# Scratch region, weight slabs, split y and weighted h placed on multiples of 128 bytes

## Chip, core and metric

The kernel runs on one core of one Trainium2 chip. The metric is the device time of one execution in microseconds, the median over runs.

## What is computed

A convolution of width 3 over two sequences of 2048 tokens and 1024 features gives 768 features; blockwise causal attention (blocks of 128 tokens, 16 heads of 64) works on them; a projection brings the result back to 1024 features, which is added to the input and normed. Then comes a dense layer of 1024x1024 with eight gated low-rank experts, again added and normed. All of it is in fp32. Cut to what matters:

```python
x = conv_general_dilated(inputs, conv_w, padding='SAME') + conv_b      # 1024 -> 768
q, k, v = split(x, 3)                    # 256 each, in blocks of 128 tokens
p = softmax(where(causal, (q@wq+bq)/8 @ (k@wk+bk).T, -1e9))
o = (p @ (v@wv+bv)) @ wo + bo
x = layernorm(inputs + o @ proj_w + proj_b)

base = x @ W_base.T + b_base
gate = softmax(x @ W_gate.T) - sigmoid(x @ W_thr.T + b_thr) / 8
weights = gate * (gate >= 0);  weights /= sum(weights)
h = einsum('nd,erd->ner', x, A)
out = layernorm(x + base + 2 * einsum('ner,ne,eor->no', h, weights, B))
```

## The kernel before

Every product is made of three fp32r matmuls (`PASSES`, line 64): each operand is split into a high part (HI, a copy in fp32r) and a low part (LO, the difference), and HI x HI, HI x LO and LO x HI are summed in one PSUM bank. The first operand of a matmul call is the one that the array holds (an LDWEIGHTS of its own), the second is the moving one, which is streamed through. TensorE runs one long stream in three stages:

1. **Convolution** (line 657). 12 sweeps of a minimal-filtering scheme over 1024-token tiles; 3456 matmuls of 256 columns. Held: the weights `w` in the arena `weights`. Moving: `x_split`, 1 KB a row, in the scratch region.
2. **Attention** (lines 1168, 1187, 1201, 1226, 1213, 1236), eight tiles of 512 tokens by eight head pairs, software-pipelined. Line 1187 makes K (bank h) and Q (bank a) with both operands in the arena; line 1236 (`add_out`) streams `heads_out`, which lies in scratch; line 1201 reads `q_and_k` and line 1226 `probs_T` and `v_heads`, all in scratch.
3. **Feed-forward** (`ffn_phase`, windows over 32 blocks of 128 tokens). A block takes 24 matmuls of each of the column groups 896 to 1161 (266 columns, banks e and h), 0 to 511 (banks c and f) and 512 to 895 (384 columns, banks d and g), all on line 1592: three passes over eight slabs `wf[kc]`. Held is `x1T` (arena), moving is the slab. Line 776 projects y: held `y_split`, moving `wp` (arena). Line 1609 applies the experts: held `h_weighted_T`, moving `wb` (arena). Lines 1582 and 1601 are transposes.

The order is written out by hand in each engine's program. SBUF is laid out by hand too. The arena `weights` starts at byte 16,512 of each partition, a multiple of 128, and `x1T`, `wp`, `wb` and the attention weights lie in it on multiples of 512 bytes from its start. `conv_tile`, `features_out`, `causal_mask` and `identity` start 96 bytes past a multiple of 128, `v_bias_rows` 32 past.

The scratch region starts at the next multiple of 32 after those (`self.base` in `AttentionStart`), which is byte 145,728: 64 bytes past a multiple of 128. `at(name, ...)` puts a tile at a byte offset in it. Nearly all offsets are multiples of 128, so most scratch tiles start 64 bytes past such a multiple; `y_split` and `proj_b_rows` start 32 past one, `weight_stage2` 96 past one.

A slab `wf[kc]` holds HI and then LO, each of `WCOLS` = 1162 columns or 4648 bytes, which is 40 bytes more than a multiple of 128. Six slabs follow each other in the arena, two (`late_weights`) in scratch. So the start of a moving read runs through many residues modulo 128: HI parts are on multiples of 16 bytes, LO parts 8 bytes past one. In slab 0 HI is on a multiple of 128 and LO 40 bytes past one. The offsets of the column groups (0, 512, 896 columns) are multiples of 128 bytes.

The LO parts of the slabs are made by GpSimd (line 956) and VectorE, the HI parts by ScalarE, once each.

Of the kernel before, what the change touches and what calls it, by code (L numbers as in the profile page):

```python
# [8 lines left out]
F32 = mybir.dt.float32  # L9
F32R = mybir.dt.float32r  # L10
# [4 lines left out]
P = 128  # L15
BATCH, SEQ, DM = 2, 2048, 1024
# [15 lines left out]
KC = WB // P  # L32
HP = HEADS // 2
XS = 3
WCOLS = DM + ER + EXPERTS + 2
GATE0 = DM + ER

BANKS = ((0, 512), (512, 896), (896, WCOLS))
QUAD = 4
# [7 lines left out]
ARENA = CC * CHUNK  # L47
MASK_ROWS = P // QUAD
MASK_STORES = QUAD
SCRATCH = 20880  # L50
SMALL = 80992
SCORE_SMALL = 81152
Phase = namedtuple("Phase", "sync gpsimd scalar vector tensor")
# [13 lines left out]
class AttentionStart:  # L67
# [9 lines left out]
    def __init__(self, ctx, nc):  # L77
        def sb(name, shape, dt):
            return ctx.enter_context(nc.sbuf_tensor(name, shape, dt))

        def sem(name):
            return ctx.enter_context(nc.semaphore(name))

        NW, TILE = self.NW, CF * ST
        self.banks = [ctx.enter_context(nc.psum_tensor(f"bank{chr(97 + i)}", [P, ST], F32)) for i in range(8)]
        self.arena = sb("weights", [P, ARENA], F32R)
        self.stages = sb("weight_stage", [P, 2 * WCOLS], F32)
        self.stage = self.stages[:, 0:NW]
        self.craw = sb("conv_tile", [P, CF, ST], F32)
        self.out = sb("features_out", [P, KC, ST], F32)  # L90
        self.mask = sb("causal_mask", [P, P], F32)
        self.ident = sb("identity", [P, P], F32)
        self.bq, self.bk = sb("q_bias", [P, HP], F32), sb("k_bias", [P, HP], F32)
        self.bv, self.bo = sb("v_bias_rows", [P, HE], F32), sb("o_bias", [P, KC], F32)

        self.start = [2 * NW * n for n in range(3)] + [6 * NW + 2 * TILE]
        self.w = [self.arena[:, a:a + 2 * NW].rearrange("p (i n) -> p i n", i=2) for a in self.start]
        self.cs = self.arena[:, 6 * NW:6 * NW + 2 * TILE].rearrange("p (i f n) -> p i f n", i=2, f=CF)

        self.bias_loaded = sem("attn_bias_loaded")  # L100
        self.wv_loaded, self.stage_loaded = sem("wv_loaded"), sem("weight_stage_loaded")
        self.w_hi, self.w_lo = sem("attn_w_hi"), sem("attn_w_lo")
        self.zeroed, self.masks = sem("attn_zeroed"), sem("attn_masks")
        self.c_loaded = sem("conv_tile_loaded")
        self.c_hi, self.c_lo = sem("conv_tile_hi"), sem("conv_tile_lo")
        self.stored = sem("stored")
        self.y_stored = [sem(f"conv_y_stored{i}") for i in range(2)]
        self.evac, self.fin_done = sem("conv_evacuated"), sem("conv_finished")

        self.base = (nc.sbuf_base + 31) // 32 * 32  # L110
        sb("scratch", [P, SCRATCH], F32)
        self.nc = nc

    def at(self, name, shape, dt, offset):

        assert 0 <= offset and offset + 4 * math.prod(shape[1:]) <= 4 * SCRATCH, name
        return self.nc.alloc_sbuf_tensor_at(name, shape, dt, offset=self.base + offset)
# [582 lines left out]
class FfnStart:  # L700
# [8 lines left out]
    def __init__(self, ctx, nc, attn, proj_w, ffn_w, lora_b):  # L709
        def sem(name):  # L710
            return ctx.enter_context(nc.semaphore(name))

        def parts(a, n):
            return attn.arena[:, a:a + 2 * n].rearrange("p (i n) -> p i n", i=2)


        qk = attn.at("q_and_k", [P, 2, 2, ST], F32, 0)
        self.k, self.q = qk[:, 0, :, :], qk[:, 1, :, :]
        late = attn.at("late_weights", [P, self.LATE * 2 * WCOLS], F32R, 45056)
        second, kept = attn.start[1], CC - self.LATE  # L720
        self.wp = [parts(attn.start[attn.WV] + 2 * DM * k, DM) for k in range(KC)]
        self.wf = [parts(second + 2 * WCOLS * k, WCOLS) for k in range(kept)]
        self.wf += [late[:, 2 * WCOLS * k:2 * WCOLS * (k + 1)].rearrange("p (i n) -> p i n", i=2) for k in range(self.LATE)]
        self.wb = parts(attn.start[attn.WO] + 2 * attn.NW, DM)

        wo = attn.start[attn.WO]
        self.x1T = attn.arena[:, wo:wo + 4 * DM].rearrange("p (i h k n) -> p i h k n", i=2, h=2, k=CC)
        self.stage = [attn.stages[:, i * WCOLS:(i + 1) * WCOLS] for i in range(2)]
        self.stage.append(attn.at("weight_stage2", [P, WCOLS], F32, 63648)[:])

        f = [(ffn_w[k], self.wf[k], WCOLS) for k in range(CC)]
        p = [(proj_w[k], self.wp[k], DM) for k in range(KC)]
        self.weights = [(lora_b, self.wb, DM)] + p + f
        self.AFTER_V, self.AFTER_QK = 1, 1 + KC
        self.KEPT = len(self.weights) - self.LATE

        raw = attn.craw[:].rearrange("p f n -> p (f n)")
        self.xt = raw[:, 0:2 * DM].rearrange("p (i n) -> p i n", i=2)
        self.yr = raw[:, 2 * DM:2 * DM + 2 * KC * P].rearrange("p (i k n) -> p i k n", i=2, k=KC)
        self.ys = attn.at("y_split", [P, 2, 2, KC, P], F32R, 68320)  # L740
        self.pb = attn.at("proj_b_rows", [P, DM], F32, 72416)

        self.w_loaded = [sem(f"ffn_w_loaded{i}") for i in range(STAGES)]
        self.w_hi = sem("ffn_w_hi")
        self.w_lo = [sem(f"ffn_w_lo{n}") for n in range(len(self.weights))]
        self.pb_loaded = sem("proj_b_loaded")
        self.x_loaded = [sem(f"x_tile_loaded{i}") for i in range(2)]
        self.y_loaded = [sem(f"y_loaded{i}") for i in range(2)]
        self.xb_ready = sem("x_plus_bias_ready")
        self.y_hi, self.y_lo = sem("y_hi"), sem("y_lo")  # L750
        self.attn_stored = attn.stored
        self.proj_done = sem("proj_done")
        self.res1_ready = sem("res1_ready")


        small = attn.at("ln_small", [P, 34], F32, SMALL)
        self.stats = small[:, 0:24].rearrange("p (k h n) -> p k h n", k=2, h=2)
        self.mv = small[:, 24:28].rearrange("p (k n) -> p k n", k=2)
        self.var_eps, self.rstd = small[:, 28:30], small[:, 30:32]
        self.minus_half, self.eps = small[:, 32:33], small[:, 33:34]  # L760
        self.consts = sem("ln_consts_ready")
        self.ln_step = [sem(f"ln{k + 1}_step") for k in range(2)]
        self.var_ready = [sem(f"ln{k + 1}_var_ready") for k in range(2)]
        self.rstd_ready = [sem(f"ln{k + 1}_rstd_ready") for k in range(2)]
        self.stats_seen = sem("ln_stats_seen")
        self.x1_ready = sem("x1_ready")
        self.first_x1 = attn.bv
# [529 lines left out]
def ffn_phase(nc, x, yT, attn, ffn, b_base, b_thr, out):  # L1297

    with ExitStack() as ctx:
# [20 lines left out]
        wts = attn.at("gate_weights", [P, EXPERTS], F32, 33536)  # L1320
        wsum = attn.at("gate_sum", [P, 3], F32, 33568)
        hw = attn.at("h_weighted", [P, ER], F32, 33600)
        hT = attn.at("h_weighted_T", [P, 2, P], F32R, 34112)
        ps_a = attn.banks[0:2]
        ps_f = [attn.banks[2:5], attn.banks[5:8]]
        HT0 = LAST
# [309 lines left out]
def build(nc, ins, out):  # L1636
    convT = nc.dram_tensor("convT_scratch", [NST, P, CF, ST], F32).ap()
    yT = nc.dram_tensor("yT_scratch", [P, KC, TOK], F32).ap()
    with ExitStack() as ctx:
        attn = AttentionStart(ctx, nc)  # L1640
        ffn = FfnStart(ctx, nc, attn, ins["proj_w"], ins["ffn_w"], ins["lora_b"])
        with ExitStack() as both:
# [27 lines left out]
            def _(pe):  # L1670
                conv.tensor(pe)
                attention.tensor(pe)

        ffn_phase(nc, ins["x"], TileColumns(yT, P), attn, ffn, ins["b_base"], ins["b_thr"], out)


# [59 lines left out]
```

## Time and profile before

| | |
|---|---|
| median of 3 runs | 1572.31 us (1571.24 to 1580.3) |
| span of the profiled execution | 1572.8 us |
| PE busy | 1541.9 us, 98% |
| PEld (weight loads) busy | 1375.7 us, 87% |
| DVE / ACT / POOL busy | 1181.8 / 610.3 / 256.3 us |
| matmuls | 10816 |
| DMA engines' time, queue q1 | 31.5% of 16 engines' span |

PE is TensorE's matmul stream and PEld its weight loads. Matmul durations overlap each other; the distance from one start to the next is what the stream takes. The chain of waits is the sequence of work that ended last, followed back from the end.

### The profile page before, as it was taken

The numbers are of one execution on the slowest core, as the hardware profiler recorded it, in microseconds if no ns is written. First come the engines' busy times: TensorE is split into PE (matmuls) and PEld (weight loads), VectorE is DVE, ScalarE is ACT, GpSimd is POOL, SyncE is SP. The second block draws the span as 40 slices with busy tenths as digits, with TensorE's granted clock in tenths as the row PEclk, the third lists the DMA queues.
The fourth block names the chain that finished last, engine by engine and source line by source line (L and its number), as shares of the span: only waits on it lengthen the run. The fifth ranks groups of instructions, "written<-read, shape, count | busy, mean of one in ns | idle before, by whom it ended". The sixth has DMA issues, their size and how long they took to land. (4 is left out here: it accounts for less than half of the span.)

```text
span 1572.8 us, 29280 instructions
## 1 busy us (share of the span) xinstructions
PE 1541.9 (98%) x10816; PEld 1375.7 (87%) x10816; DVE 1181.8 (75%) x2792; ACT 610.3 (39%) x1732; POOL 256.3 (16%) x227
## 2 busy tenths in 40 slices
PE   7999999999999999999999999999999999999997
PEld 7999999999878888888888887898988999989987
DVE  8859967887876666666666677787788888788875
ACT  4224223322466767676676677211111111111110
POOL 0000000000000101010000113433333333333331
PEclk9999999999999999999999999999999999999999
DMA  8987774678810100101010222312211112211111
GB/s 323 370 308 272 257 256 166 240 279 282 280 68 1 55 20 34 53 0 53 0 53 0 76 93 77 108 61 74 76 61 60 60 60 75 75 60 60 60 55 44
DMA packets 55301, 181.05 MB, mean 115 GB/s; under 512 B 5568, under 2 KB 13888, under 8 KB 48704
## 3 DMA queue, kind: packets, MB, share of 16 engines
q1 hardware_dynamic: 53504, 173.81, 31.5%
q10 hardware_dynamic: 1728, 6.29, 1.0%
q8 instruction: 47, 0.77, 0.2%
q14 instruction: 22, 0.18, 0.0%
HBM read 125.49 MB, written 54.53 MB: 114 GB/s over the span
## 5 line engine op out<-in xcount | busy, mean ns | idle before, releaser
L976 ACT ACTIVATE scores_and_probs<-scores_and_probs,score_neg_max 128x128 f32<-128x128 f32 x512 | 198.0, 391 | 2.1 <-DVE score_neg_max L1077 2.1
L943 POOL TENSOR_TENSOR weights<-conv_tile,weights 128x1024 fp32r<-128x1024 f32 x14 | 35.7, 2552 | 860.7 <-ACT weights L962 775.7
L1072 DVE CUSTOM_DVE_ANT_0 scores_and_probs<-bankb,causal_mask 128x128 f32<-128x128 f32 x256 | 59.2, 288 | 114.6 <-PE bankc L1201 114.2
L1428 ACT ACTIVATE gate_exp<-h_and_gate,gate_neg_max 128x8 f32<-128x8 f32 x32 | 9.7, 302 | 347.9 <-DVE gate_neg_max L1503 347.9
L380 ACT ACTIVATE x_split<-x_planes 128x1024 fp32r<-128x1024 f32 x47 | 49.9, 1061 | 169.6 <-PE bankf L657 126.7
L1168 PE MATMUL bankg<-weights 128*128 128x512 f32 x378 | 103.2, 408 | 0.6 <-DVE v_heads L1062 0.5
L1187 PE MATMUL bankh<-weights 128*128 128x512 f32 x384 | 99.0, 393 | 1.7 <-DVE probs_T L1090 1.7
L1187 PE MATMUL banka<-weights 128*128 128x512 f32 x384 | 98.3, 391 | 0.8
L976 ACT ACTIVATION_READ_ACCUMULATOR scores_and_probs<-scores_and_probs,score_neg_max 128x1 f32 x512 | 97.5, 190 | 0.0
L511 DVE TENSOR_TENSOR x_split<-x_planes,x_split 128x1024 fp32r<-128x1024 f32 x47 | 57.4, 1222 | 49.8 <-ACT x_split L380 49.8
L657 PE MATMUL banka<-x_split,weights 128*128 128x256 f32 x576 | 77.8, 283 | 13.2 <-DVE weights L615 8.7
L1187 PEld LDWEIGHTS bankh<-weights 128*128 128x128 f32 x384 | 71.6, 188 | 19.6 <-DVE probs_T L1090 2.9
L1187 PEld LDWEIGHTS banka<-weights 128*128 128x128 f32 x384 | 71.5, 188 | 18.6 <-POOL weights L943 3.4
L793 DVE BATCH_NORM_STATS2 ln_small<-residual_sum 128x6 f32<-128x512 f32 x126 | 81.1, 686 | 5.9 <-DVE residual_sum L787 4.6
L657 PEld LDWEIGHTS banka<-x_split,weights 128*128 128x128 f32 x576 | 72.1, 192 | 14.0 <-issue 12.0
L1084 DVE TENSOR_TENSOR scores_and_probs<-scores_and_probs,prob_inv_sum 128x1024 f32<-128x1024 f32 x64 | 80.4, 1256 | 2.2
L1201 PEld LDWEIGHTS bankb<-q_and_k 64*128 64x128 f32 x512 | 61.7, 187 | 22.6 <-issue 22.6
L1168 PEld LDWEIGHTS bankg<-weights 128*128 128x128 f32 x378 | 66.3, 189 | 12.3 <-DVE v_heads L1062 1.2
L802 DVE TENSOR_SCALAR out_tile<-residual_sum,ln_small 128x1024 f32<-128x1024 f32 x32 | 76.0, 2376 | 1.0 <-POOL ln_small L809 1.0
L657 PE MATMUL bankb<-x_split,weights 128*128 128x256 f32 x576 | 76.7, 281 | 0.0
L657 PE MATMUL bankc<-x_split,weights 128*128 128x256 f32 x576 | 75.7, 278 | 0.0
L657 PE MATMUL banke<-x_split,weights 128*128 128x256 f32 x576 | 75.5, 278 | 0.0
(244 smaller groups left out, 3885.0 us busy)
## 6 DMA issues: line engine op xcount, KB each, us to landing
x_raw<-in_xT SPq DMA_DIRECT2D x31, 1028.0 KB, 7.1
conv_tile<-in_x SPq DMA_DIRECT2D x32, 512.0 KB, 3.6
out<-out_tile SPq DMA_DIRECT2D x32, 512.0 KB, 2.7
conv_tile<-convT_scratch SPq DMA_DIRECT2D x16, 768.0 KB, 6.5
ce_scratch<-conv_l SPq DMA_DIRECT2D x16, 512.0 KB, 7.5
x_planes<-ce_scratch SPq DMA_DIRECT2D x16, 512.0 KB, 4.9
conv_y<-in_conv_w SPq DMA_DIRECT2D x6, 1152.0 KB, 6.5
convT_scratch<-conv_y SPq DMA_DIRECT2D x12, 512.0 KB, 6.1
```

Of the source, the lines that this page charges most:

```text
L380: nc.scalar.activation(xs[:, j % XS, HI], T[:, j % 2, 0:2], ACT.Copy).then_inc(x_hi, 1)
L511: nc.vector.tensor_tensor(xs[:, j % XS, LO], T[:, j % 2, 0:2], xs[:, j % XS, HI].bitcast(F32), ALU.subtract).then_inc(x_lo, 1)
L657: last = nc.tensor.matmul(acc[f][:, k, :], w[:, c, a, k, f * P:(f + 1) * P], xs[:, j % XS, b, k, c % CPG, :], start=(c == 0 and k == 0 and ...
L793: nc.vector.bn_stats(self.stats[:, k, h, :], src[:, h * ST:(h + 1) * ST]).then_inc(step, 1)
L802: nc.vector.tensor_scalar(dst, src, self.mv[:, k, 0:1], self.rstd[:, k:k + 1], ALU.subtract, ALU.mult).then_inc(ready, 1)
L943: nc.gpsimd.tensor_tensor(cs[:, LO, a:b, :], craw[:, a:b, :], cs[:, HI, a:b, :].bitcast(F32), ALU.subtract).then_inc(c_lo, 1)
L976: last = nc.scalar.activation(probs[:, s % 2, i, :], probs[:, s % 2, i, :], ACT.Exp, bias=ntop[:, s % 2, i:i + 1], scale=SCORE_SCALE, accu ...
L1072: last = nc.vector.tensor_tensor_reduce(out=probs[:, s % 2, i, :], in0=ps_s[h][:, n * P:(n + 1) * P], in1=mask[:], scale=1.0, scalar=LOWES ...
L1084: nc.vector.tensor_tensor(probs[:, s % 2, :, :], probs[:, s % 2, :, :], inv[:, s % 2, :].unsqueeze(2).broadcast_to([P, 2 * BLK, P]), ALU.m ...
L1168: last = nc.tensor.matmul(bank[:], cs[:, a, V[0] + kc, b * P:(b + 1) * P], wqkv(attn.WV, c, kc, cols), start=(i == 0), stop=(i == 5))
L1187: last = nc.tensor.matmul(out[:], wqkv(weight, a, kc, slice(s * P, (s + 1) * P)), cs[:, c, part[0] + kc, :], start=(i == 0), stop=(i == 5))
L1201: last = nc.tensor.matmul(ps_s[j][:, cols], q[rows(j), s % 2, cols], k[rows(j), s % 2, cols], start=True, stop=True)
```

## The change

`self.base` is rounded up to a multiple of 128: it becomes byte 145,792, and every scratch tile moves up by 64 bytes. The slabs' parts get a pitch `WPITCH` of 1184 columns (4736 bytes, 37 times 128), of which the first 1162 are used, so that HI and LO of all eight slabs start on multiples of 128. `weight_stage2`, `y_split` and `proj_b_rows` move up because the late slabs are longer, to multiples of 128. `h_weighted_T` moves by 64 bytes relative to the region, and so stays on a multiple of 128. `v_heads`, `q_and_k`, `probs_T`, `heads_out`, `x_split` and the other tiles that were 64 bytes past a multiple of 128 are on one now; a few small ones (`score_neg_max`, `h_weighted`, `gate_inverses`) were on one and are 64 past it now. `conv_tile`, `identity` and `v_bias_rows` stay. No engine's list of instructions differs: same operations, shapes, order and waits.

```diff
@@ -34,6 +34,8 @@
+LINE = 128
+WPITCH = (4 * WCOLS + LINE - 1) // LINE * LINE // 4
@@ -47,7 +49,7 @@
-SCRATCH = 20880
+SCRATCH = 20864
@@ -107,8 +109,8 @@
-        self.base = (nc.sbuf_base + 31) // 32 * 32
-        sb("scratch", [P, SCRATCH], F32)
+        self.base = (nc.sbuf_base + LINE - 1) // LINE * LINE
+        sb("scratch", [P, SCRATCH + LINE // 4], F32)
@@ -716,17 +718,20 @@
-        late = attn.at("late_weights", [P, self.LATE * 2 * WCOLS], F32R, 45056)
+        def slab(region, k):
+            return region[:, 2 * WPITCH * k:2 * WPITCH * (k + 1)].rearrange("p (i n) -> p i n", i=2)[:, :, 0:WCOLS]
+
+        late = attn.at("late_weights", [P, self.LATE * 2 * WPITCH], F32R, 45056)
         second, kept = attn.start[1], CC - self.LATE
-        self.wf = [parts(second + 2 * WCOLS * k, WCOLS) for k in range(kept)]
-        self.wf += [late[:, 2 * WCOLS * k:2 * WCOLS * (k + 1)].rearrange("p (i n) -> p i n", i=2) for k in range(self.LATE)]
+        assert second + 2 * WPITCH * kept <= attn.start[attn.WO]
+        self.wf = [slab(attn.arena[:, second:], k) for k in range(kept)] + [slab(late, k) for k in range(self.LATE)]
-        self.stage.append(attn.at("weight_stage2", [P, WCOLS], F32, 63648)[:])
+        self.stage.append(attn.at("weight_stage2", [P, WCOLS], F32, 64000)[:])
@@ -737,8 +742,8 @@
-        self.ys = attn.at("y_split", [P, 2, 2, KC, P], F32R, 68320)
-        self.pb = attn.at("proj_b_rows", [P, DM], F32, 72416)
+        self.ys = attn.at("y_split", [P, 2, 2, KC, P], F32R, 68736)
+        self.pb = attn.at("proj_b_rows", [P, DM], F32, 72832)
@@ -1320,7 +1325,7 @@
-        hT = attn.at("h_weighted_T", [P, 2, P], F32R, 34112)
+        hT = attn.at("h_weighted_T", [P, 2, P], F32R, 34176)
```

## Rows read from the trace of the kernel before

**Rows 1.** The page: busy time and share of the span, then TensorE's granted clock.

```profile
PE 1541.9 (98%) x10816; PEld 1375.7 (87%) x10816; DVE 1181.8 (75%) x2792; ACT 610.3 (39%) x1732; POOL 256.3 (16%) x227
...
PEclk9999999999999999999999999999999999999999
```

**Rows 2.** Waits of PE: who was waited for, total us, times, longest us.

```profile
PE banka L657 <- DVE weights L615: 8.7, 1, 8.7
PE banka L1582 <- PEq L1642: 3.3, 1, 3.3
PE banka L657 <- ACT conv_m L414: 3.2, 1, 3.2
PE bankd L1226 <- DVE heads_out L1094: 2.3, 1, 2.3
```

**Rows 3.** The chain of waits inside one feed-forward block: start us, us, what.

```profile
1173.72 3.04 PE banke L1592 x24
1176.75 5.55 PE bankc L1592 x24
...
1185.39 2.09 PE bankd L1592 x12
1187.48 1.40 PE banka L776 x6
1188.88 1.39 PE bankb L776 x6
1190.28 0.70 PE bankc L1609 x3
1190.97 0.53 PE bankd L1609 x3
```

**Rows 4.** Timeline of PE in attention: start us, us (overlapping), line, operation.

```profile
599.92 0.86 PE L1236 MATMUL banke<-heads_out,weights 128*128 128x512 f32 x3
600.62 0.86 PE L1236 MATMUL bankf<-heads_out,weights 128*128 128x512 f32 x3
601.32 1.54 PE L1187 MATMUL bankh<-weights 128*128 128x512 f32 x6
602.70 1.52 PE L1187 MATMUL banka<-weights 128*128 128x512 f32 x6
```

**Rows 5.** Instructions of lines 1592 and 1609: duration ns min/median/max.

```profile
L1592 PE MATMUL bankc<-weights x288: 389/394/400, 996.0 to 1541.7; 128*128 128x512 f32 x144
L1592 PE MATMUL bankd<-weights x288: 332/337/423, 1002.3 to 1547.3; 128*128 128x384 f32 x144
L1592 PE MATMUL bankd<-late_weights,weights x96: 331/334/338, 1005.7 to 1548.3; 128*128 128x384 f32 x96
L1609 PE MATMUL bankc<-weights,h_weighted_T x48: 389/395/398, 1009.5 to 1549.0; 128*128 128x512 f32 x48
```

**Rows 6.** Windows over two stretches of the convolution, line 657: PE busy (matmuls), clock, DMA.

```profile
45.00:145.00 100.00, 100.00 (x851) 1.00 0.83 311
175.00:275.00 100.00, 100.00 (x885) 1.00 0.67 240
```

**Rows 7.** Timeline of PE around an early wait of the convolution.

```profile
17.02 0.84 PE L657 MATMUL banke<-x_split,weights 128*128 128x256 f32 x6
17.70 0.84 PE L657 MATMUL bankf<-x_split,weights 128*128 128x256 f32 x6
19.12 0.97 PE L657 MATMUL banka<-x_split,weights 128*128 128x256 f32 x6 [0.58 <-DVE x_split L511]
19.93 0.87 PE L657 MATMUL bankb<-x_split,weights 128*128 128x256 f32 x6
20.64 0.87 PE L657 MATMUL bankc<-x_split,weights 128*128 128x256 f32 x6
```

**Rows 8.** Groups by line and shape on the other engines: busy us, mean ns | idle before.

```profile
L983 ACT ACTIVATE probs_T<-banka 128x512 f32<-128x512 f32 x64 | 38.2, 597 | 3.9 <-PE banka L1213 3.9
L1441 ACT ACTIVATE weights<-banka 128x512 fp32r<-128x512 f32 x32 | 19.1, 597 | 88.5 <-PE banka L1582 88.5
L1094 DVE TENSOR_TENSOR heads_out<-bankd,heads_out 128x512 fp32r<-128x512 f32 x64 | 43.5, 680 | 0.0
L1538 DVE TENSOR_TENSOR weights<-bankb,weights 128x512 fp32r<-128x512 f32 x32 | 21.8, 681 | 0.1
```

**Rows 9.** Weight loads of lines 776 and 1592: duration ns min/median/max.

```profile
L776 PEld LDWEIGHTS banka<-weights,y_split x180: 187/188/188, 1006.5 to 1531.4; 128*128 128x128 f32 x180
L1592 PEld LDWEIGHTS bankc<-weights x288: 187/188/193, 995.9 to 1541.5; 128*128 128x128 f32 x144
```

## The prediction

> **What bounds the kernel.** I read the busy times first [rows 1]: PE 98% of the span at full clock in every slice, DVE 75%, ACT 39%. The whole kernel is one TensorE stream, and the named waits of PE [rows 2] come to under 20 us, 8.7 of them the start. So the time is the sum of the distances between matmul starts, and the question of this change is a narrow one: does the distance depend on where the operands start modulo 128 bytes? Everything else in the program is the same. I looked next at the chain inside one feed-forward block [rows 3], because it gives that distance free of overlap (time of a piece over its count), then at attention's timeline [rows 4], and last at the convolution [rows 6, 7].
>
> **The slabs, 2304 matmuls, the part that moves most.** Three widths, 768 matmuls each.
> - 512 columns: 24 in 5.55 us, 231 ns each [rows 3]. These reads start at all sorts of residues. The same width with the moving operand on multiples of 128 already: line 776, 6 in 1.40 and 6 in 1.39 us, 233 and 232 ns; line 1609, 3 in 0.70 us, 233 ns [rows 3]; K on line 1187, from 601.32 to 602.70 us for 6, 230 ns [rows 4]. Aligned neighbours stand at -1 to +2 ns: -0.8 to +1.5 us over 768.
> - 384 columns: 12 in 2.09 us, 174 ns; aligned on line 1609, 3 in 0.53 us, 177 ns [rows 3]. The two late slabs, in another place and with other residues, have a median duration 3 ns below the kept ones (334 against 337) [rows 5]. So -2.3 to +2.3 us over 768.
> - 266 columns: 24 in 3.04 us, 127 ns [rows 3]. No aligned row has this width. The nearest rate is the convolution's, 256 columns in 113.0 ns (100 us over 885) or 117.5 ns (100 over 851) [rows 6], which scaled to 266 columns gives 117 or 122 ns: a bound of -10 ns or -7.5 us if alignment were all that parts them. But the convolution's moving operand is itself 64 bytes off, so its faster rate speaks for the shape of the stream, not for alignment. I take 0, and keep -7.5 as the low end.
>
> The strongest row for zero is inside the group: the 288 kept matmuls of bank c have durations from 389 to 400 ns over all residues, and the 48 of line 1609, all on multiples of 128, from 389 to 398, with medians 394 and 395 [rows 5]. If the start mattered, the first group would be wider or later; it is neither beyond 2 ns. Slabs together: 0, from -10.6 to +3.8 us.
>
> The Trainium skill, page "Advanced Engine Details and Errata", section SBUF Cachelines, says that SBUF is read in lines of 16 bytes, that consecutive accesses in a line run at full rate, and that changing line each access is penalised. By that rule a LO slab, 8 bytes into a line, would touch one line more in some 128, and an estimate from it is under 1% of 231 ns, 2 ns on 768 of the 2304 matmuls, 1.5 us; the rows above leave room for no more than that. The page "SBUF — State Buffer", section Operand start alignment, asks of an operand only that it start on a multiple of its element size, and says that this is legality and was not timed; the spread of 389 to 400 ns agrees with there being nothing large.
>
> **Attention.** `heads_out` on line 1236 is streamed 64 bytes off: from 599.92 to 600.62 us for 3, 233 ns; K, aligned, 230 ns [rows 4]. If all of that were alignment: 384 matmuls by 3 ns, -1.2 us. It also equals the aligned 232 and 233 ns of lines 776 and 1609, so I take 0. For `q_and_k`, `v_heads` and `probs_T` no aligned row of that shape exists; the widths are 64 and 128 columns, where the weight load is the longer half, and loads last 188 ns from `y_split` (32 bytes off) as from `x1T` (on a multiple of 512 from the arena's start) [rows 9]. I take 0; the 1.2 us stands for the bound.
>
> **The other engines.** ACT writes 512 columns to `probs_T` (64 off) and to the arena (aligned) in 597 ns both; DVE's low part takes 680 ns into `heads_out` (64 off) and 681 into the arena [rows 8]. So their instructions cost the same, and PE, not they, carries the time: 0. Were a DVE instruction to gain some ns it would lie behind PE's stream; only the waits of rows 2 and the last block's end would see it, under 1 us.
>
> **The convolution** is where the trace shows something that is no function of addresses. The stream runs 851 matmuls in 100 us in one stretch and 885 in another, with the same residues and the clock at 1.00 in both [rows 6]. The change from fast to slow stands at a wait: six matmuls start 0.68 us apart before 19.12 us (17.02 to 17.70) and 0.71 us apart after it (19.93 to 20.64) [rows 7], and it is fast again at the latest from 175 us. I read this as a phase between weight loads and matmuls that a restart picks, and that then holds. From 19.1 us to about 172 us the slow stretch has some 1300 matmuls, and costs 1300 x 4.5 ns = 5.9 us. The rest of the stage, to 415 us, has 3456 - 1300 - 80 = about 2080 matmuls at the fast rate. Transfers are behind other waits here, not ahead of the stream, and the move by 64 bytes changes nothing that I can tie to the choice, but a few ns in an early load or mix may. Sum: 0, with -5.9 (all fast) and +9.4 us (2080 x 4.5, slow to the end) as ends.
>
> **Sum** against the profiled execution's own 1572.8 us: slabs 0, attention 0, other engines 0, convolution 0. Its time is 0.5 us above the median of the runs, so the forecast is 1572. The sum of low ends is -10.6 - 1.2 - 5.9 = -18 us (1554), of high ends +3.8 + 9.4 = +13 us (1585).
>
> **Rivals.**
> - *Alignment helps the slabs.* 2304 matmuls by 4.5 ns, the size of the one step between two rates that the trace has: -10.4 us, 1562. For it: the 266-column group is 5 to 10 ns above the scaled rate of the convolution. Against: lines 776 and 1609. Chance 0.12.
> - *Alignment helps every stream that was off*, the convolution's 3456 and line 1236's 384 too: 6144 x 4.5 = -27.6 us, 1545. Against: `heads_out`, 64 off, equals aligned rows, and the convolution has its fast rate already at 64 off. Chance 0.05.
> - *The convolution is all fast*: -5.9 us, 1567. Chance 0.10.
> - *The convolution stays slow*, the rival on the other side: a restart near 172 us or 300 us picks the slow phase; from there each matmul costs 4.5 ns more, up to +9.4 us, 1582. It decides only where the slow rate is held past both restarts. For it: one of the few restarts did go that way; and the third run of before, 1580.3, is 8 us up. Chance 0.13, and 0.02 more that slabs land on a slow pattern as well, 5 ns on 2304 = 11.5 us, 1593.
> - *No change* within the two rates: 0.58.
>
> **The numbers.** A measurement of this kernel can tell about 1%, 16 us, from no change. Faster by over 1% needs the second rival or the first with a fast convolution: 0.06. Slower by over 1% needs the last case of the slow rival: 0.02. Same: 0.92. The range of 8 in 10 reaches to the first rival and to the slow convolution: 1561 to 1582.
>
> **What would show it.** In the changed kernel's chain, 24 matmuls of bank c in 5.5 to 5.6 us, 12 of bank d in 2.05 to 2.15, 24 of bank e in 3.0 to 3.1; line 1236 at 0.70 us for three; ACT at 597 and DVE at 680 ns. The windows 45 to 145 us and 175 to 275 us would show 851 or 885, or two other counts if alignment acts there. I am wrong if 24 of bank c take under 5.45 us, if 24 of bank e fall under 2.9 us, or if a width of the convolution's rate appears that is neither 113 nor 117.5 ns.

## The result, and the profile after

| | before | changed |
|---|---|---|
| median | 1575.71 us (8 runs, 1571.24 to 1580.89) | 1582.55 us (8 runs, 1581.35 to 1583.56) |
| span of the profiled execution | 1572.8 us | 1581.0 us |

The ratio is 1.0048, 95% interval 1.0032 to 1.0064: slower, by about 7 us. The spread is a finding in itself: the kernel before has runs 10 us apart, the changed one stays within 2.2 us. The forecast of 1572 started from the median of three runs of the kernel before, 1572.31 us; over eight runs it is 1575.71, so 3.4 us of the distance between forecast and result belong to the kernel before.

Where did it go? The first and last starts of the stages tell (instructions by line, duration ns min/median/max, first and last start us). The changed kernel:

```profile
L659 PE MATMUL bankf<-x_split,weights x576: 279/283/283, 14.6 to 426.9; 128*128 128x256 f32 x192
L1597 PE MATMUL banke<-weights x288: 279/284/334, 1001.8 to 1545.3; 128*128 128x266 f32 x144
```

and the same line of the convolution before (bank f; its first feed-forward matmul starts at 993.1 us):

```profile
L657 PE MATMUL bankf<-x_split,weights x576: 276/276/281, 13.6 to 414.8; 128*128 128x256 f32 x192
```

So the convolution ends at 426.9 us where it ended at 414.8, with its first matmul at 8.5 and 8.7 us: 12.3 us longer. From there to the first matmul of the feed-forward it is 574.9 us against 578.3, 3.4 less; from there to the end 579.2 against 579.7, 0.5 less. The three and 0.2 at the start sum to the +8.2 us of the spans.

The windows over the convolution, in the changed kernel (columns as in [rows 6]):

```profile
45.00:145.00 100.00, 100.00 (x835) 1.00 0.82 301
175.00:275.00 100.00, 99.94 (x833) 1.00 0.65 227
330.00:390.00 60.00, 60.00 (x503) 1.00 0.82 287
```

835 matmuls in 100 us are one every 119.8 ns; [rows 6] had 117.5 and 113.0. (A window counts the matmuls that overlap its ends too, so its rate comes out 0.2 to 0.5 ns below the one from start to start: 120.0 ns here, 117.8 and 113.3 in the kernel before.) The rate is new, and between the short waits it is the same in all three windows. The timeline that answers to [rows 7] has groups of six 0.71 to 0.73 us apart, with no restart needed to bring them there:

```profile
16.02 0.88 PE L659 MATMUL bankb<-x_split,weights 128*128 128x256 f32 x6
16.73 0.88 PE L659 MATMUL bankc<-x_split,weights 128*128 128x256 f32 x6
17.45 0.88 PE L659 MATMUL bankd<-x_split,weights 128*128 128x256 f32 x6
18.18 0.88 PE L659 MATMUL banke<-x_split,weights 128*128 128x256 f32 x6
```

Attention, to be laid beside [rows 4]. `heads_out` now takes 0.68 us for three (227 ns, it was 233), and K behind it 1.36 us for six (227, it was 230), though both operands of K lie in the arena and have not moved:

```profile
593.47 0.84 PE L1241 MATMUL banke<-heads_out,weights 128*128 128x512 f32 x3
594.15 0.84 PE L1241 MATMUL bankf<-heads_out,weights 128*128 128x512 f32 x3
594.83 1.52 PE L1192 MATMUL bankh<-weights 128*128 128x512 f32 x6
596.19 1.52 PE L1192 MATMUL banka<-weights 128*128 128x512 f32 x6
```

The feed-forward's chain, beside [rows 3], is the old one to 0.03 us a piece, though every part of a slab but the very first has moved:

```profile
1182.42 3.01 PE banke L1597 x24
1185.43 5.55 PE bankc L1597 x24
...
1191.85 2.10 PE bankd L1597 x12
...
1196.17 1.40 PE banka L781 x6
```

And PE's waits in the convolution got smaller (those of [rows 2] are 8.7 and 3.2), as they do behind a slower stream:

```profile
PE banka L659 <- DVE weights L617: 8.5, 1, 8.5
PE banka L659 <- ACT conv_m L416: 0.8, 1, 0.8
```

### The profile page after: what moved, and what is told of

Its sections match the earlier page's. It is cut to its first block and busy times, and to the rows that moved or that the text cites. A ratio compares the mean times of both kernels' runs of the same rounds, so it can differ in the third digit from the quotient of the medians.

```text
span 1581.0 us, 29280 instructions
## 1 busy us (share of the span) xinstructions
PE 1554.3 (98%) x10816; PEld 1391.6 (88%) x10816; DVE 1182.1 (75%) x2792; ACT 610.2 (39%) x1732; POOL 256.3 (16%) x227
## 5 line engine op out<-in xcount | busy, mean ns | idle before, releaser
L659 PE MATMUL bankc<-x_split,weights 128*128 128x256 f32 x576 | 79.0, 284 | 0.0
L659 PE MATMUL bankd<-x_split,weights 128*128 128x256 f32 x576 | 79.0, 284 | 0.0
L659 PE MATMUL bankf<-x_split,weights 128*128 128x256 f32 x576 | 78.4, 283 | 0.0
```

What stands on the lines that cost most here:

```text
L659: last = nc.tensor.matmul(acc[f][:, k, :], w[:, c, a, k, f * P:(f + 1) * P], xs[:, j % XS, b, k, c % CPG, :], start=(c == 0 and k == 0 and ...
```

## The experiments

Sixteen kernels, each run beside the kernel before on the same chip, three rounds each. "Distance" below is the start of the moving tile `x_split` minus the start of the held weights' arena, modulo 256 bytes; all held and moving pieces of the convolution lie at multiples of 512 and 1024 bytes from these two starts, so one number holds for all 3456 pairs. Before it is 192, in the changed kernel 0. "Rate" is the mean distance in time between matmul starts in the convolution, from windows as above or from the starts of the 72 matmuls of one step of a sweep (the table below has the latter). Each kernel has one trace, of one execution; the medians are over all its runs.

### Which part of the change

**e1_scratch64**, the changed kernel with the region back:

```diff
-        self.base = (nc.sbuf_base + LINE - 1) // LINE * LINE
+        self.base = (nc.sbuf_base + 31) // 32 * 32
```

> The changed kernel with the scratch region back at 64 bytes past a multiple of 128; the slabs keep their pitch of 1184 columns. In the changed kernel's trace every one of the convolution's 3456 matmuls starts 120 ns after the last, before it was 118 and then 113, and the convolution is 12 us longer. Theory A (the place of the scratch region does it, because the moving operand x_split starts on a multiple of 128 like the held weights): the convolution is at 113 or 118 ns again, 406 to 412 us long, heads_out at 233 ns, and the time is 1571 to 1581 us. Theory B (the slab pitch or the place of the slabs does it): nothing comes back, 1581 to 1584 us.

**e2_base_only**, the kernel before with the region alone moved:

```diff
-        self.base = (nc.sbuf_base + 31) // 32 * 32
+        self.base = (nc.sbuf_base + 127) // 128 * 128
```

> The kernel before with the scratch region alone moved to a multiple of 128 (byte 145,792), slabs at their old pitch. Theory A: the convolution at 120 ns throughout, 418 us long, heads_out at 227 ns, 1581 to 1584 us. Theory B: 1571 to 1581 us, convolution at 113 or 118 ns. Theory C (a restart picks a phase at random, and the changed kernel only fell on a bad one): the convolution shows 113 or 118 ns in at least part of its length, whatever the place.

e2 took 1584.13 us (0.1 us above the range of theory A), ratio 1.0061 (1.0044 to 1.0078); e1 1576.69 us, ratio 1.0013 (1.0000 to 1.0025). Windows of e2, then of e1:

```profile
45.00:145.00 100.00, 100.00 (x836) 1.00 0.81 302
175.00:275.00 100.00, 100.00 (x836) 1.00 0.63 226
```

```profile
45.00:145.00 100.00, 100.00 (x851) 1.00 0.84 311
175.00:275.00 100.00, 100.00 (x852) 1.00 0.65 230
```

Theory A holds and B falls: the region's place alone brings the loss. e1 is at 117.8 ns from its first restart, near 19 us, to the end, where the profiled execution before fell to 113.3 at 172 us, with the same distance: at 192 two rates are possible. (The traced execution of e1 is the slowest of its ten, 1582.55 us, so it may not be typical.)

The slab pitch was the part that I had priced most carefully. The times do not resolve it: e2 and the changed kernel are 1.6 us apart, with overlapping intervals of their ratios. The traces show more. From the first matmul of the feed-forward to the end it is 581.1 us in e2 (region moved, old pitch) and 580.9 in e1 (new pitch, old region), against 579.7 before and 579.2 with both. In e2 24 matmuls of bank c take longer than the 5.55 us of both other kernels:

```profile
1184.96 5.58 PE bankc L1592 x24
```

So the places of the feed-forward's tiles are worth up to 1.9 us there; which pair of operands does it was not tested (`y_split` and `h_weighted_T` differ between e2 and the changed kernel too).

### Which tile, and whether it is the place or the distance

**e3_conv64** moves `x_split` and the tiles behind it by 64 bytes in the changed kernel; the phase mask goes to the end of the region to make room.

```diff
-    xs = attn.at("x_split", [P, XS, 2, 2, CPG, UQ], F32R, 12288)
+    xs = attn.at("x_split", [P, XS, 2, 2, CPG, UQ], F32R, 12288 + 64)
```

> The changed kernel with x_split and the convolution tiles behind it (conv_m, conv_l, conv_y, x_raw) moved up by 64 bytes, all else as in the changed kernel; of these TensorE reads only x_split. Theory A: the convolution is back at 113 or 118 ns while heads_out keeps 227 ns and attention its 575 us: 1568 to 1577 us, under both kernels. Theory A' (not x_split, but the tiles of the other engines in scratch): x_planes alone would still be aligned and the convolution would stay near 120 ns. Theory C: between 1569 and 1582 us with no relation to the place.

**e4_arena64** leaves `x_split` where the change put it and moves the arena:

```diff
+        sb("spacer", [P, 16], F32)
         self.arena = sb("weights", [P, ARENA], F32R)
```

> The changed kernel with a spacer of 64 bytes ahead of the arena, so that everything held or streamed from the arena (convolution and attention weights, slabs, x1T) starts 64 bytes past a multiple of 128, and x_split and the rest of scratch on multiples of 128. Theory R (what counts is the distance between the held and the moving operand modulo 128): the convolution is at 113 or 118 ns as before, 406 to 412 us, heads_out at 233 ns, and 1572 to 1581 us. Theory M (what counts is where the moving operand starts): 120 ns and 418 us stay, heads_out at 227 ns, 1581 to 1584 us, perhaps with K, Q and V slower, whose moving operand is now 64 off.

e3 1576.62 us (ratio 1.0017, 1.0008 to 1.0027), e4 1576.56 (1.0011, 0.9997 to 1.0024). Windows of e4:

```profile
45.00:145.00 100.00, 100.00 (x884) 1.00 0.87 324
175.00:275.00 100.00, 100.00 (x884) 1.00 0.67 239
```

e4 decides for theory R: `x_split` lies where it does in the changed kernel, and the rate is not 120 but 113.3 ns, because the held operand has moved. The same trace has `heads_out` back at 0.70 us for three, though it too lies where the change put it:

```profile
598.05 0.86 PE L1242 MATMUL banke<-heads_out,weights 128*128 128x512 f32 x3
598.75 0.86 PE L1242 MATMUL bankf<-heads_out,weights 128*128 128x512 f32 x3
```

So a distance of 0 is bad for the 256-column stream (120 against 113 or 118 ns) and good for the 512-column one of `heads_out` (227 against 233, at 192).

The distance of its own operands is not all that sets a stream's rate. In no kernel here does the distance between K's two operands change, as both lie in the arena. Yet K's median group of six runs at 230 ns where `heads_out`, just ahead of it, runs at 233 (before, e1, e4), and at 227 where `heads_out` runs at 227 (changed, e2, e3). K seems to take its rate over from the stream ahead of it. My hope for e3, a time under both kernels, failed: its convolution held 117.8 ns from about 18 us on (852 and 851 in the two windows), and what attention gained was lost to that.

### The distances one by one

**e5_conv32** and **e6_conv96** are e3 with 32 and 96 for 64. **e7_conv16** to **e11_conv112** start `x_split` inside a longer tile, so that it alone has the odd residue (16, 8, 48, 80 and 112 bytes); **e12_conv128** is the control with 128. Shown for e11:

```diff
-    xs = attn.at("x_split", [P, XS, 2, 2, CPG, UQ], F32R, 12288)
+    xs_tile = attn.at("x_split", [P, XS * 4 * CPG * UQ + 32], F32R, 12288)
+    xs = xs_tile[:, 28:28 + XS * 4 * CPG * UQ].rearrange("p (x i k c n) -> p x i k c n", x=XS, i=2, k=2, c=CPG)
```

> The changed kernel with x_split and the convolution tiles behind it 32 bytes past a multiple of 128 (the run before had 64 bytes). So far a distance of 0 modulo 128 between held and moving operand gave 120 ns throughout, a distance of 64 gave 113 or 118 ns by stretches. Theory R128 (the distance counts modulo 128 and only 0 is the bad one): 113 or 118 ns, no 120, 1572 to 1579 us. Theory R64 (what counts is a half of 128, 0 against 64): 32 lies between and shows a rate of its own, either side of 120. Theory P (any distance other than 0 leaves the choice to the restarts): two rates or more in one trace.

> The same with 96 bytes, which is 32 bytes short of the next multiple of 128. If only the size of the distance counts, the rates are those of the run at 32. If its sign counts (which of the two reads is ahead), they differ, and one of the two may hold 113 ns throughout, which would be 1565 to 1572 us with attention at its 575 us.

> The changed kernel with x_split alone started 16 bytes into its tile, which starts on a multiple of 128; the tiles behind it are moved by 32 bytes to make room. Theory R128: not 120 ns but 113 or 118. Theory W (reads collide while they are within one 32-byte or 64-byte piece of each other): still 120 ns, 418 us for the convolution, 1581 to 1584 us. It also settles whether x_split is the tile, since no other tile that TensorE reads in the convolution moves.

> The same with 8 bytes, the distance that the LO slabs of the kernel before had from a multiple of 16. Theory W: 120 ns stay. Theory R128: 113 or 118 ns. Theory L (a start within a line of 16 bytes costs each read one more line): over 120 ns by 1 to 3 ns, 1584 to 1593 us.

> The changed kernel with x_split alone 48 bytes past a multiple of 128 (the tiles behind it 128 bytes up, which is no change modulo 128). Distances of 16, 32 and 64 gave 1576 us with rates of 113 to 118 ns and a switch of rate at restarts in some; 0 and 96 gave 1582 us. Theory S (the sign counts: a moving operand that starts 16 to 64 past the held one is good, one that starts just short of it is bad): 1574 to 1578 us, rates of 113 to 118 ns. A distance that holds 113 ns throughout would give 1566 to 1571 us and beat the kernel before.

> The same with 80 bytes, 48 short of the next multiple. Theory S: between 64 (1576) and 96 (1582), a mean rate of 117 to 120 ns. If the rates depended on the distance's size alone, it would equal the run at 48 within 1 us.

> The same with 112 bytes, 16 short of the next multiple. Theory S: as bad as 96 or 0, 1580 to 1584 us, 119 to 121 ns on average. Size alone: like 16, 1574 to 1578 us.

> Control: x_split and the tiles behind it moved up by 128 bytes, the same layout modulo 128 as the changed kernel. If the distance modulo 128 is the cause, 120 ns throughout and 1581 to 1584 us. If moving those tiles or the phase mask mattered in itself, or the modulus were larger than 128, the convolution would leave 120 ns.

| distance | kernel | rate by stretch, ns | median us | ratio (95%) |
|---|---|---|---|---|
| 0 | changed | 120.0 | 1582.55 | 1.0048 (1.0032 to 1.0064) |
| 8 | e8 | 120.0, then 116.7 | 1595.74 | 1.0153 (1.0096 to 1.0210) |
| 16 | e7 | 118.7, then 113.3 | 1575.73 | 1.0012 (0.9993 to 1.0030) |
| 32 | e5 | 116.7, 117.8, 116.7 | 1575.91 | 1.0014 (1.0000 to 1.0027) |
| 48 | e9 | 118.3 | 1577.87 | 1.0025 (1.0010 to 1.0041) |
| 64 | e3 | 117.8 | 1576.62 | 1.0017 (1.0008 to 1.0027) |
| 80 | e10 | 120.0, then 118.3 | 1580.57 | 1.0039 (1.0023 to 1.0055) |
| 96 | e6 | 120.0 | 1581.69 | 1.0057 (1.0041 to 1.0073) |
| 112 | e11 | 113.3 | 1566.81 | 0.9947 (0.9929 to 0.9964) |
| 128 | e12 | 118.7 | 1578.80 | 1.0034 (1.0020 to 1.0049) |
| 192 | before, e1, e4 | 117.8 and 113.3; 117.8; 113.3 | 1573 to 1577 | |

Three things follow. First, it is `x_split` and nothing else in the region: e9, e10 and e11 have every other tile in the same place and differ only in where `x_split` starts inside its tile, and their rates are 118.3, then 120.0 and 118.3, and 113.3. (e7 moves `x_split` by 16 bytes and the tiles behind it, none of which TensorE reads, by 32, and the rate leaves 120.) Second, the two named rules that I had tried to fit fall. By "the sign counts" (S) 112 was to be as bad as 0, and it is the best of all. By "only 0 is bad, in a period of 128" (R128) 96 should have left 120 and the control at 128 should have been at 120, and neither is so. Third, in these traces a rate changes only where the stream restarts after a pause, the shortest of them 0.27 us (before, at 172 us); many pauses leave it as it is. In e7 that is a wait of 1.56 us near 320 us:

```profile
320.58 1.60 PE L660 MATMUL banka<-x_split,weights 128*128 128x256 f32 x12 [1.56 <-ACT conv_m L417]
322.02 1.52 PE L660 MATMUL bankb<-x_split,weights 128*128 128x256 f32 x12
```

with 845 matmuls in 100 us before it and 532 in 60 after it:

```profile
175.00:275.00 100.00, 100.00 (x845) 1.00 0.64 229
330.00:390.00 60.00, 60.00 (x532) 1.00 0.86 298
```

The best distance, e11:

```profile
45.00:145.00 100.00, 100.00 (x885) 1.00 0.87 323
175.00:275.00 100.00, 100.00 (x885) 1.00 0.67 238
```

e8's time is inconclusive: its four runs took 1580.19, 1602.94, 1603.0 and 1588.55 us, and the traced one is the fastest (span 1578.4 us), so the trace cannot explain the median.

### The period, and the good place once more

**e13_conv256** and **e14_conv512** have `x_split` 256 and 512 bytes up; **e15_held64_176** has the arena 64 up and `x_split` 176 up, which is distance 112 again; **e16_conv624** has it 624 up, 112 + 512.

> The changed kernel with x_split alone 256 bytes up (the tiles behind it 1024 up). Theory M256 (the rate depends on the distance between held and moving operand modulo 256): 120 ns throughout and 1581 to 1584 us, as at 0. Theory M512: another rate, as at 128 (118.7 ns, 1579 us) or elsewhere. Theory N (any move draws a new rate): nothing can be said beforehand, 113 to 120 ns.

> The same with 512 bytes, the step between neighbouring held tiles. Theories M256 and M512: 120 ns throughout, 1581 to 1584 us. Theory N: any rate.

> Arena 64 bytes up, x_split 176 up, so that their distance is that of the run at 112, which held 113.3 ns; all other distances are those of the run with the arena alone moved, with attention at 580 and the feed-forward at 572 us. Theory R (distance): 113.3 ns throughout, convolution about 403 us, 1571 to 1575 us. Theory M (x_split's own place): the rate is not that of the run at 112; 1576 to 1586 us.

> x_split 624 bytes up, 112 + 512. If the rate repeats with 512 or a divisor: 113.3 ns throughout and 1565 to 1568 us, the second layout that beats both kernels. If the run at 112 was luck: 117 to 120 ns and 1574 to 1583 us.

e13 1582.82 us, ratio 1.0044 (1.0029 to 1.0059), and e14 1582.06, 1.0039 (1.0024 to 1.0054), both at 120: the rate of distance 0 is back at 256 and 512, with 128 in between not showing it. 256 is thus the period as far as tried: from 0 at 256 and 512, from 112 at 512 alone. e15 1572.34 us, 0.9980 (0.9970 to 0.9989); e16 1568.19 us, 0.9951 (0.9935 to 0.9967). Windows of e13, e12, e15 and e16, in this order:

```profile
45.00:145.00 100.00, 100.00 (x836) 1.00 0.82 304
175.00:275.00 100.00, 100.00 (x836) 1.00 0.62 226
```

```profile
45.00:145.00 100.00, 100.00 (x845) 1.00 0.83 305
175.00:275.00 100.00, 100.00 (x845) 1.00 0.64 229
```

```profile
45.00:145.00 100.00, 100.00 (x885) 1.00 0.88 323
175.00:275.00 100.00, 100.00 (x885) 1.00 0.67 239
```

```profile
45.00:145.00 100.00, 100.00 (x885) 1.00 0.86 323
175.00:275.00 100.00, 100.00 (x885) 1.00 0.67 239
```

Theory N (each move draws its rate anew) would have to bring back by chance 120 twice and 113.3 twice, and 113.3 throughout is a rate that of the nine distances from 0 to 112 only one has. e15 gives the distance theory its second test from the held side: two starts that differ from those of e11, the same distance, the same rate. It also shows attention paying at the other end (578.3 us between the stages, e11 575.0).

**e11 and e16 beat both kernels**, e11 by 0.53% against the kernel before, and so does e15, by 0.2%. The rate alone would give more: 3456 x (120.0 - 113.3) ns is 23 us against the changed kernel, and the convolution got 15.7 us shorter. The quicker stream catches up with its feeders. PE's waits in e11:

```profile
PE banka L660 <- DVE x_split L514: 2.8, 3, 1.5
PE banka L660 <- ACT conv_m L417: 2.6, 1, 2.6
```

## Why the prediction was wrong, step by step

I had forecast 1572 us, no change within 1%, in a range of 1561 to 1582. The change is indeed under 1%, but the median lies 0.6 us above the range, and the sign is that of the rival on the slow side, whose mechanism (a chance restart) was not the one at work. "Same within 1%" came true, but by luck as much as by reason: the term taken as 0 with the least ground was 12.3 us. The prediction's own sign of being wrong, a rate in the convolution that is neither 113 nor 117.5 ns, is what the changed kernel shows.

- **The question, where the operands start modulo 128, with everything else the same.** The question was put wrongly. Every comparison that I made set moving operands with different residues side by side. What counts in the convolution is where the held and the moving operand start relative to each other, modulo 256 as far as the runs go. Line 1236 and line 776 gave 233 ns each for different pairs, and I took the agreement for independence. K's 230 ns, which I used as an aligned row, goes up and down with `heads_out` ahead of it, so it told nothing of K's own place.
- **Convolution, 0 with ends of -5.9 and +9.4 us.** This is the step that failed: measured +12.3 us. I saw the two rates of [rows 6, 7] and read them rightly as a phase that a restart picks (e7 and the kernel before show it; e1 and e4, with the same distance, each hold one of them from 19 us on). The error was to treat 113 and 117.5 as the whole list. The sentence "the move by 64 bytes changes nothing that I can tie to the choice" had no row behind it: the trace has one distance only in this stage. With 120 ns the upper end would have been 2080 x 7 + 1300 x 2.5 = 18 us, of which waits give some back.
- **Slabs, 0, from -10.6 to +3.8.** Right in size: 5.55, 2.10 and 3.01 us where 5.55, 2.09 to 2.11 and 3.04 stood; the feed-forward with the tail is 0.5 us shorter. The reason, that the place does not matter, is too strong: with only the region or only the pitch changed this stretch is 1.4 and 1.2 us longer (e2, e1).
- **Attention, 0, at most -1.2.** Too small: -3.4 us, nearly three times the bound. `heads_out` fell from 233 to 227 ns (384 x 6 = 2.3 us), below the 230 that I had taken for the best an aligned stream can do, and K behind it from 230 to 227 (about 0.7 us).
- **Other engines, 0.** Right: ACT's copy into `probs_T` takes 598 ns (597), DVE's low part 680 ns (680) in the changed trace.
- **The page on lines of 16 bytes** (the Trainium skill, "Advanced Engine Details and Errata", SBUF Cachelines) played no part that a run shows: e8, 8 bytes into a line, begins at the same 120.0 ns as distance 0 and goes on at 116.7. As e8 changes the distance too, it does not test that page by itself.
- **Chances.** 0.58 for "no change within the two rates" was too much for a stage with 3456 matmuls, one distance and two rates already in one trace.

The runs show that the convolution's rate depends on the distance, comes back after 256 bytes where that was tried, and may change at a restart. That the weight loads and the moving reads get in each other's way in the memory is how I read it; no record shows a read. The Trainium skill, page "TensorE: Matmul & The Clock Gate", section "Step-by-step: what each phase is for", has two independent read ports for the two operands and says that loading the next weights takes no read bandwidth from the running matmul. The runs here agree with that only in part: if the two reads had nothing to do with each other, the place of the held operand should not matter to the stream, and moving only the arena, with the instructions unchanged, took it from 120 to 113 ns, 6% (e4).

What stays open: why 112 holds 113.3 ns and its neighbours do not, whether the distance alone counts at every value (only 112 was had from two pairs of starts modulo 256 with one steady rate), which rate a restart picks where more than one is seen (8, 16, 32, 80, 192), what carries the rate from `heads_out` to K, which tiles cost the feed-forward its 1 to 2 us in e1 and e2, the distances from 129 to 255 other than 192, and where e8's median of 1595.74 us comes from.

## What to carry to other kernels

Where TensorE is the bound, alignment of a tile is not a goal in itself: compare the start-to-start time of one line's matmuls over stretches and layouts, and try a few offsets of the moving tile against the held one. A price of zero for a move needs a row that has both places; rows that agree for other pairs of operands don't give it. When one trace shows two rates for the same instructions, take the list of rates as open, and do not take its spread as the most that a change of layout can do.

## What was not expected of the hardware

- The same 256-column fp32r stream runs at mean rates of 113.3, 116.7, 117.8, 118.3, 118.7 and 120.0 ns a matmul at a granted clock of 1.00, by the distance of its two operands and, at one distance, by what a restart picks.
- The rate is kept for hundreds of matmuls and changes at a restart. That may be why the kernel before scatters by 10 us from run to run and the changed one, with one rate, by 2.2 (e11, with one rate too, by 1.5). It is not shown, as only one execution of each was traced; e12, whose trace has one rate too, has runs from 1576.07 to 1583.62 us.
- The same distance is good for one width and bad for another: 0 gives 120 ns for 256 columns and 227 for the 512 of `heads_out`, 192 gives 113 or 118 and 233.
